# Compressed interaction network in float32 on one core: the 64-row leftovers multiplied as four 64x64 tiles in place of two 64x128 tiles

## What is computed

```
x0 = prev = r_inputs                               # (2048, 39, 16)
for i in 0, 1, 2:                                  # h = 39, 64, 64
    Wr = W_i.reshape(h, 39, 128)
    z = relu(einsum('bhk,bmk,hmf->bfk', prev, x0, Wr) + b_i)
    results.append(z[:, :64]);  prev = z[:, 64:]
y = sum(concat(results, axis=1), axis=-1) @ W_lin  # (2048, 1)
```

## Time and profile before

| | us |
|---|---|
| median of 3 runs (2027.6 to 2028.27) | 2027.66 |
| the profiled execution | 2026.19 |
| its span, first to last instruction | 2024.4 |
| TensorE matmul busy | 2002.4 |
| VectorE busy | 1790.8 |
| ScalarE busy | 518.0 |

### The profile page before, as it was taken

How to read it: one execution, slowest core, us unless ns; L and a number is a source line. 1 busy time by engine, 2 the same in 40 slices (tenths; PEclk the granted TensorE clock), 3 DMA queues, 4 the chain that set the end, 5 groups by cost and what they waited for, 6 DMA issues and landing times.

```text
span 2024.4 us, 19227 instructions
## 1 busy us (share of the span) xinstructions
PE 2002.4 (99%) x6042; PEld 806.0 (40%) x6042; DVE 1790.8 (88%) x1181; ACT 518.0 (26%) x482; POOL 1.2 (0%) x5
## 2 busy tenths in 40 slices
PE   7999999999999999999999999999999999999998
PEld 2344333443334443334433344333444333443342
DVE  6988988889888899888898888998888988889988
ACT  1321233311333112332123331133321233311331
POOL 0000000000000000000000000000000000000000
PEclk8999999999999999999999999999999999999999
DMA  7978766678666687666786667876667866678710
GB/s 200 196 151 181 170 154 134 152 160 192 146 142 151 141 190 173 138 144 147 168 189 143 147 142 149 192 161 147 139 151 171 177 153 137 150 153 192 156 27 0
DMA packets 98552, 309.03 MB, mean 153 GB/s; under 512 B 19252, under 2 KB 19252, under 8 KB 98408
## 3 DMA queue, kind: packets, MB, share of 16 engines
q1 hardware_dynamic: 97400, 307.71, 69.4%
q10 hardware_dynamic: 1136, 1.12, 0.2%
HBM read 308.74 MB, written 0.01 MB: 153 GB/s over the span
## 4 chain that ended last, share of the span: by engine, by line
PE 96%; DVE 2%; issue 1%; ACT 0%; DVEq 0%
PE acc L384 67%; PE acc L424 25%; PE acc L378 3%; DVE prod L243 1%; PE acc L433 1%; DVE x_bc L213 1%; DVE prod L249 0%; PE acc_y L476 0%; DVE x_rot L228 0%; DVE sum L291 0%; ACT res L516 0%; DVE x_seed L366 0%; DVE pool L311 0%; DVE prod L247 0%; DVEq L309 0%
## 5 line engine op out<-in xcount | busy, mean ns | idle before, releaser
L243 DVE TENSOR_TENSOR prod<-prev,x_bc 128x2048 f32<-128x2048 f32 x512 | 1138.4, 2282 | 4.3 <-PE acc L384 4.3
L384 PE MATMUL acc<-prod,w_sb 128*128 128x512 f32 x2432 | 1053.1, 594 | 2.3 <-DVE prod L243 2.3
L384 PEld LDWEIGHTS acc<-prod,w_sb 128*128 128x128 f32 x2432 | 459.1, 190 | 594.1 <-issue 569.2
L424 PE MATMUL acc<-prod,w_sb 128*64 128x512 f32 x2432 | 530.0, 594 | 1.4 <-DVE prod L243 1.4
L486 ACT ACTIVATE prev<-acc,bias 64x1024 f32<-64x1024 f32 x128 | 142.0, 1109 | 1320.5 <-PE acc L384 1319.7
L384 PE MATMUL acc<-x_rot,w_sb 117*128 117x512 f32 (+1 forms) x768 | 338.2, 596 | 7.4 <-DVE x_rot L228 7.4
L424 PEld LDWEIGHTS acc<-prod,w_sb 128*64 128x64 f32 x2432 | 171.2, 137 | 356.1 <-issue 302.2
L491 ACT ACTIVATE prev<-acc,bias 32x1024 f32<-32x1024 f32 x256 | 283.2, 1106 | 4.1
L249 DVE TENSOR_TENSOR prod<-prev,x_bc 128x1024 f32<-128x1024 f32 x192 | 228.6, 1217 | 1.5
L228 DVE TENSOR_TENSOR x_rot<-x_rot,x_rep 117x1024 f32<-117x1024 f32 (+1 forms) x192 | 221.0, 1218 | 8.0 <-DMA x_rot<-x 8.0
L384 PEld LDWEIGHTS acc<-x_rot,w_sb 117*128 117x128 f32 (+1 forms) x768 | 146.0, 191 | 195.4 <-issue 182.6
(11 more groups left out here) (23 smaller groups left out, 87.4 us busy)
## 6 DMA issues: line engine op xcount, KB each, us to landing
x_bc<-x SPq DMA_DIRECT2D x310, 256.0 KB, 10.5
x_bc<-x SPq DMA_DIRECT2D x155, 512.0 KB, 18.5
x_rot<-x SPq DMA_DIRECT2D x192, 312.0 KB
x_rot<-x SPq DMA_DIRECT2D x192, 156.0 KB
x_bc<-x SPq DMA_DIRECT2D x124, 128.0 KB, 6.4
x_rep<-x SPq DMA_DIRECT2D x64, 192.0 KB
x_rep_s<-x SPq DMA_DIRECT2D x64, 128.0 KB, 21.9
x_rot_s<-x SPq DMA_DIRECT2D x64, 128.0 KB, 21.9
```

What stands on the lines that cost most here:

```text
L243: mul = nc.vector.tensor_tensor(prod[:, s:s + w, :], twice, x_bc[:, u, t:t + w, :], ALU.mult)
L384: mm = nc.tensor.matmul(acc[:, h, :], w, rhs[:, BANK * h:BANK * h + BANK], start=start, stop=stop)
L424: mm = nc.tensor.matmul(acc2[HALF * h:HALF * h + HALF, u, :], w2_sb[:, ORDER[pos], :], prod[:, pos % RING, BANK * h:BANK * h + BANK], star ...
```

## The change

`split` now loops over two halves of the outputs inside its loop over the column halves. Each of its matmuls contracts 64 rows to 64 outputs: rows 0 to 63 or 64 to 127 of the array's input side, and output partitions 0 to 63 or 64 to 127. The same products are multiplied with the same weights into the same places of PSUM; two matmuls of 64x128 become four of 64x64, in the order (h, o) = (0, 0), (0, 1), (1, 0), (1, 1). The semaphore increment on a split's last matmul stays where it was.

Ahead of each split TensorE's queue gets an increment of a new semaphore, `left_asked`. No engine waits for it. It stands between the waits and the first matmul.

```
+        left_asked = sem("left_asked")
...
                 for h in range(NH):
                     k = slice(HALF * h, HALF * h + HALF)
-                    mm = nc.tensor.matmul(acc[:, h, :], w[k, :], rhs[h], start=start, stop=stop)
+                    for o in range(2):
+                        f = slice(HALF * o, HALF * o + HALF)
+                        mm = nc.tensor.matmul(acc[f, h, :], w[k, f], rhs[h], start=start, stop=stop)
                 return mm
...
             def layer0_split(i):
                 pe.wait_ge(prod0_ready, i * (C0 + 1) + 1)
+                pe.sem_inc(left_asked, 1)
                 split(acc0, w0_sb[:, C0, :], [x_rot_s[0:HALF, :], x_rot_s[HALF:P, :]],
                       True, False).then_inc(split_used, 1)
...
                     if pos == 0:
+                        pe.sem_inc(left_asked, 1)
                         split(acc1, w1_sb[:, c, :], [prod[0:HALF, s, 0:BANK], prod[HALF:P, s, BANK:NB]],
                               True, False).then_inc(chunk_used, 1)
```

## The result

The changed kernel takes 2022.74 us (median of 11 runs, 2021.36 to 2023.62), the kernel before 2027.5 us (11 runs, 2025.59 to 2030.01). The ratio is 0.9978, with a 95% interval of 0.9970 to 0.9986: the medians are 4.8 us apart, and the interval stands for a gain of 2.8 to 6.1 us. The gain is small, but its interval leaves out zero.

The account below looks back on a forecast made before the run. TensorE's chain of matmuls was taken to bound the kernel from 54.4 us. Savings of 15 x 0.20 + 15 x 0.04 + 2 x 0.04 = 3.7 us, off 2027.66, gave 2024.0 us; range 2022.5 to 2027.8.

Parts of the forecast that it names:

- The bound: From 54.4 us to the end of the last block's layer 1, time saved between TensorE's matmul starts is saved at the end.
- The seams: Pairs of splits save 0.20 us behind layer2_left and 0.04 us behind layer 2, 15 times each.
- an emptying: The last round before another tile shape is some 0.10 to 0.11 us longer, as the array empties.
- an exposed load: The first round after a shape change shows its weight load: 0.05 us for 64 columns, 0.105 for 128.
- The increment: left_asked ahead of each split: taken as costing nothing, with up to 0.6 us kept for the range.
- the tight seam: Split behind layer 2, its product ending 0.24 us before the matmuls; 0.10 us left after a 0.14 us hand-over.
- VectorE's lead: VectorE keeps up: 0.24 us stays behind layer 2, and the next products have 0.5 us of slack.
- 1: The increment ahead of each split empties the array: 10 to 19 us slower, 2034 to 2043 us; chance 10%.
- 2: Start of a new group with a wait, not shape, empties the array: 2.4 us less gain, 2026.4 us; chance 12%.
- 3: Weight loads of 64x64 tiles are not hidden: 5 to 11 us, 2029 to 2035 us; chance 5%.
- 4: The four tiles of a split don't run side by side: 53 us more, 2077 us; chance 3%.
- the likeliest case: The 3.7 us gain less at most 0.6 us at one kind of seam: 2022.8 to 2025.5 us, 70%.

Follow-up runs that it names:

- the two with 128x64 chunks: Changed kernel with full chunks of layers 1 and 0 as 128x64 pairs: 2018.36 us; also with VectorE's layer-0 split product moved behind the layer-1 split's: 2017.62 us.
- the increments alone: Changed kernel with its splits put back to two 64x128 tiles, left_asked increments kept: 2027.25 us, ratio 1.0002 to the kernel before.
- the two half-changes: Increments in, 64x64 tiles only in layer 0's splits: 2032.24 us, ratio 1.0024 to before; only in layer 1's splits: 2028.93 us, ratio 1.0010.
- the other order: Changed kernel with the loop over output halves outside that over row halves: 2023.0 us, ratio 0.9981 to the kernel before.
- VectorE's order: Changed kernel with VectorE's product for the layer-0 split moved behind the product of the layer-1 split: 2023.47 us, ratio 0.9981 to before.

## Why the prediction was right, point by point

*The bound.* It was right that time saved between two matmul starts after 54 us is saved at the end: the stretch shrank by what the seams shrank.

*The seams.* 0.20 and 0.04 us per seam were forecast, 2.94 - 2.74 = 0.20 and 1.92 - 1.87 = 0.05 measured (0.04 by the unrounded starts), and the sum of 3.7 is 3.70 in the stretch. The two terms behind it, an emptying of 0.10 to 0.11 us and an exposed load of 0.05 or 0.105, also gave the sizes of other kernels that arrange them differently: +4.8 expected and +4.79 measured, +2.4 and +2.37. For the two with 128x64 chunks they gave a ratio of 0.995 to 0.9965 and one of about 0.9953, and 0.9959 and 0.9954 were measured; there the wait for VectorE was an allowance, not a sum.

*The increment.* Taken at nothing, and it is nothing: alone, in 608 copies in mid-stream, and with the lead at the tight seam raised. That it can have a price where TensorE's queue has no lead was right as well. But the price that I worked out for eight, 15 us, was less than half of the 34.0 measured, since I let those of the second split run while the first one's matmuls were still to be handed on.

*VectorE's lead.* The 0.10 us left at the tight seam sufficed. With the seam 0.15 us closer to the end of layer 1, in the kernel with 128x64 chunks, it no longer did, and the product came late as worked out from the same rows.

*The rivals.* 1 fell to the increments alone, 2 to the two half-changes, 3 to the weight loads and the other order, 4 to the timeline: eight records take 0.86 us in the middle of the stream (1032.70 to 1033.56), two rounds of 0.43. The Trainium skill (TensorE: Matmul & The Clock Gate, "Part 3") says in its list of what overlaps that weight loads overlap only with matmuls of another row group. That is not what this chip did: four loads of 0.15 us in all ran under matmuls on the same rows. Above that list the same part of the Trainium skill also lets a load into a background weight buffer run ahead; no row here tells where a load goes. The Trainium skill (TensorEngine Tiling (Array Packing), "Key Properties") says that changing the tiling mode drains TensorE and changing only the tile doesn't. The two half-changes agree: each further change of shape costs 0.16 us, which I divide into 0.11 us for the last round and 0.05 us for the load.

*The time.* 2024.0 was forecast and 2022.74 measured, 2022.99 in the repetition. The gain of 3.7 us was right, but the nearness of the time itself is partly luck. What comes before the stretch varies: the stretch began anywhere from 53.6 to 56.1 us in these traces, which alone is 2.5 us. The forecast's allowance for the spread was 0.6 us, taken from three runs; eleven runs of the changed kernel spread over 2.3 us and eleven of the kernel before over 4.4. So 2022.74 lies within the range of 2022.5 to 2027.8, but just under the 2022.8 to 2025.5 given to the likeliest case. Faster by over 0.2% was given 0.28, and no clear difference 0.55; the ratio came out at 0.9978, the repetition at 0.9981, on either side of that line.

*Not tried:* the 64x64 tiles without any increment ahead of them.

## What to carry to other kernels

Where TensorE bounds a kernel, look for the places where neighbouring matmuls differ in tile shape. Each cost 0.15 to 0.21 us here, and this went when both sides had one shape, even at twice as many instructions. Judge a tile shape with its neighbours: each half of this change lost time by itself. When an effect is as small as the runs' spread, measure a stretch of the trace between two fixed events: here it repeated to 0.03 us, where whole runs of one kernel spread over up to 4.4 us.

## What was unexpected

A queue entry of 0.151 us costs nothing in one place and much in another. 608 of them in a stream left the stretch at 1932.28 us (1932.31 without), while 14 more per block at the splits, where TensorE's queue has little lead, cost 34.0 us, half of their 32 x 14 x 0.151 = 68 us. And the stretch came out at 1932.31 us in four executions of three kernels (the changed one twice, the other order, VectorE's order), on a program whose whole runs vary by 2 us and more.
